# Lookup exponentials moved to GpSimd, and the layer-3 attention summary computed with values as weights in two 64-column tiles

## The reference, cut to what matters

```python
# L2F: product-key lookup of experts
h = silu(x @ W_up.T + b_up) @ W_down.T + b_down
q = (h @ W_q.T)...                        # 2 halves, 8 heads, 64 wide
sim = q . keys                            # 45 keys in each half
scores, idx = top_k(sim, 8)               # in each half
sc, pk = top_k(all 64 sums of a pair, 8)  # 8 experts in each of 8 heads
z = h . down_embed[indices]
z = silu(z * softmax(sc))
x = x + sum over heads, k of z * up_embed[indices]

# L3X: linear attention over the context; 16 heads of 16, 64 features
q', k' = relu(q @ Wqf.T), relu(k @ Wkf.T) * mask
kv, k_sum = sum over tokens of k' v, sum over tokens of k'
out = (q' kv) / (q' k_sum + 1e-8)
x = x + out @ Wo.T + bo
```

## Time and profile before

| | |
|---|---|
| median of 3 runs | 1339.32 us (1335.14 to 1339.72) |
| profiled execution, its time | 1336.76 us |
| its span | 1334.9 us |
| mean granted clock of TensorE | 0.919 of full speed |
| busy: TensorE, its weight loads | 1140.2 us (85%), 817.2 us (61%) |
| busy: DVE, ScalarE, GpSimd | 696.4 (52%), 482.1 (36%), 165.4 (12%) |
| this stage (L2F and L3X) | about 847 to 1161 us of the span |

### The profile page before, as it was taken

One profiled execution on the slowest core, in us unless ns is written; L12 is line 12 of the kernel. 1 busy time (PEld: TensorE's weight loads), 2 busy tenths in 40 slices (PEclk: granted clock), 3 DMA queues, 4 the chain that ended last, 5 costly groups with the idle time before them and its releaser, 6 DMA issues.

```text
span 1334.9 us, 22850 instructions
## 1 busy us (share of the span) xinstructions
PE 1140.2 (85%) x9353; PEld 817.2 (61%) x9353; DVE 696.4 (52%) x1532; ACT 482.1 (36%) x1069; POOL 165.4 (12%) x168
## 2 busy tenths in 40 slices
PE   6987889977877999999999977856986976777998
PEld 5866556656654555555556655735764755676886
DVE  3543456763326777655666253462626647374332
ACT  1101146762312355655566833222332321121322
POOL 0004000000001000000000000073635462000000
PEclk9998999998987999999999999977978957786999
DMA  9021200003003000000000020152524241003552
GB/s 365 1 95 48 111 1 1 2 2 154 0 16 135 1 2 2 1 2 1 2 2 2 2 77 1 54 145 63 152 70 123 78 113 48 14 0 158 198 204 81
DMA packets 16182, 84.38 MB, mean 63 GB/s; under 512 B 3152, under 2 KB 3664, under 8 KB 12368
## 3 DMA queue, kind: packets, MB, share of 16 engines
q1 hardware_dynamic: 7888, 57.75, 11.3%
q0 software_dynamic: 8192, 25.17, 6.7%
HBM read 82.65 MB, written 0.26 MB: 62 GB/s over the span
## 4 chain that ended last, share of the span: by engine, by line
PE 74%; DVE 12%; issue 5%; ACT 4%; another core or an unknown queue 3%; POOL 1%; DMA 1%; POOLq 0%; SPq 0%; DVEq 0%; ACTq 0%
PE L2X_bank_ring L1762 6%; PE L2X_bank_ring L1778 6%; PE L2X_bank_read L1792 5%; PE L2X_bank_ring L1701 4%; PE L2F_bank_sim L2389 3%; PE L1X_banks_scores L910 3%; PE L2X_bank_ring L1710 2%; PE L1X_bank_proj L887 2%; PE L0X_bank_k L457 2%; PE L2F_bank_keys L2347 2%; PE L3F_bank_y L3327 2%; PE L0X_bank_moments L468 2%; PE L2F_banks_pair L2364 2%; PE L3F_bank_gathered L3276 2%
## 5 line engine op out<-in xcount | busy, mean ns | idle before, releaser
L2059 DVE TENSOR_REDUCE L2X_max_parts<-L2X_bank_ring 128x1 f32<-128x512 f32 x256 | 158.3, 684 | 85.7 <-PE L2X_bank_ring L1762 85.7
L1970 ACT ACTIVATE L2X_context_exp<-L2X_bank_ring 128x384 f32<-128x384 f32 (+1 forms) x384 | 144.5, 465 | 62.1 <-PE L2X_bank_ring L1778 59.5
L2477 POOL DMA_INDIRECT L2F_rows<-in_L2F_embed_dram,L2F_expert x128 | 132.3, 1033 | 107.8 <-DVE x L2698 50.4
L1762 PE MATMUL L2X_bank_ring<-L2X_context_kT,L2X_q_masked 32*128 32x512 f32 x512 | 96.9, 630 | 0.0
L1016 ACT ACTIVATE L1X_probs<-L1X_clipped,L1X_drop,L1X_keep 128x1024 f32<-128x1024 f32 x64 | 77.9, 1240 | 32.1 <-DVE L1X_clipped L1075 24.9
L2389 PEld LDWEIGHTS L2F_bank_sim<-L3X_v_ones,L3X_k_features 128*128 128x128 f32 x512 | 72.1, 211 | 26.0 <-issue 24.2
L1075 DVE TENSOR_SCALAR L1X_clipped<-L1X_banks_scores 128x1024 f32<-128x1024 f32 x64 | 75.4, 1220 | 24.1 <-PE L1X_banks_scores L910 22.3
L2389 PE MATMUL L2F_bank_sim<-L3X_v_ones,L3X_k_features 128*128 128x34 f32 x512 | 69.2, 285 | 20.0 <-issue 19.8
L1778 PE MATMUL L2X_bank_ring<-L2X_q_and_max,L2X_context_kT 32*128 32x384 f32 (+1 forms) x768 | 86.0, 497 | 0.0
L1792 PEld LDWEIGHTS L2X_bank_read<-L2X_context_exp,L2X_context_v_ones 128*32 128x32 f32 x2048 | 50.2, 109 | 43.8 <-issue 33.4
L1792 PE MATMUL L2X_bank_read<-L2X_context_exp,L2X_context_v_ones 128*32 128x128 f32 x2048 | 75.8, 277 | 1.1 <-ACT L2X_context_exp L1970 0.8
(11 more groups left out here) (618 smaller groups left out, 2075.6 us busy)
## 6 DMA issues: line engine op xcount, KB each, us to landing
L3F_expert_weights<-in_L3F_experts_dram SPq DMA_DIRECT2D x16, 1280.0 KB, 5.6
L1A_groups<-in_L1A_groups_dram SPq DMA_DIRECT2D x3, 1536.0 KB, 9.6
ctxT<-in_ctxT_dram SPq DMA_DIRECT2D x8, 512.0 KB, 10.5
L0X_tokens<-in_L0X_tokens_dram SPq DMA_DIRECT2D x8, 512.0 KB, 15.0
slot<-in_L1A_dram SPq DMA_DIRECT2D x1, 3584.0 KB, 11.4
slot<-in_L0F_dram SPq DMA_DIRECT2D x1, 3072.0 KB, 11.0
slot<-in_L2A_dram SPq DMA_DIRECT2D x1, 3072.0 KB, 10.8
slot<-in_L2F_dram SPq DMA_DIRECT2D x1, 2476.5 KB, 9.7
```

The costliest lines, as they stand in the source:

```text
L1762: nc.tensor.matmul(bank[:, :], qm[32 * g:32 * g + 32, b, c, j, :], cT[32 * g:32 * g + 32, s % 3, blk * 512:(blk + 1) * 512], start=True, s ...
L1970: nc.scalar.activation(ex[:, n % NE, g, 0:width(s)], bank_of(s_e, done(n) + g + 1)[:, 0:width(s)], ACT.Exp, scale=SCALE).then_inc(s_e, 1)
L2059: nc.vector.tensor_reduce(parts[:, j, g, blk:blk + 1], bank_of(s_ft, n)[:, :], AX, ALU.max).then_inc(s_ft, 1)
L2477: pool.indirect_dma_start(out=rows[:, r, k, :], out_offset=None, in_=env.dram["L2F_embed"], in_offset=bass.IndirectOffsetOnAxis(idx[:, b, ...
```

## The change

1. GpSimd computes the exponentials of z and of the softmax of the second element, as powers of a constant exp(-1) (`per_e`): `tensor_tensor(..., ALU.pow)`. `exp_z(n-2)` stands after the fourth gather of chunk n. ScalarE keeps the first element's softmax at step 0. The sign of the shifted scores is turned for that.
2. The buffers of z, exp(z) and weights become three deep; DVE does `products(m)` before `weighted_sum(m-1)`.
3. The ring uses three buffers for nine chunks, then four. `choose(*parts[2])` moves to m = 6, `choose(*parts[3])` to m = 9; FRONT becomes 2.
4. `summary` has the 34 columns of values and ones of a pair as weights, in column tile 0 or 64 by turns, and moves the pair's 128 features. At an element's end ScalarE copies the bank (`copy_kv`), TensorE turns it (`turn_kv`, 4 transposes), and `kv_blocks` reads the turned form. Wv is packed so that pairs lie together.
5. TensorE no longer waits for the last `s_z`; 10 idle products instead of 24. The pieces 5 and 6 of element 0 move behind step 31, between those of element 1, and so do `divided(0)` and `add_out(0)` on DVE. `norm3` is split (`moments3`).

The diff, cut to its core:

```diff
-    ring = [0, 1, 2, 0, 1, 2, 3] + [n % 4 for n in range(len(chunks) - 7)]
+    ring = [n % 3 for n in range(9)] + [(n + 3) % 4 for n in range(len(chunks) - 9)]
...
-    FRONT, FINISH = 3, 25
-    exp_after = {1: 0, 4: 1, 6: 2, 8: 3, 13: 4, 16: 5, 17: 6, 21: 7, 23: 8, 25: 9, 26: 10, 27: 11, 29: 12, 31: 13}
+    FRONT, FINISH = 2, 25
...
-            vp = vo[:, n % NB, :].rearrange("p (a u c e) -> p a u c e", a=2, u=2, c=4)
             for j in range(NPAIR):
-                c, ct = divmod(j, 4)
-                i = nc.tensor.matmul(bank_kv[b][:, j * 2 * VW:(j + 1) * 2 * VW], kf[:, n % NB, j, :, :].rearrange("p r f -> p (r f)"),
-                                     vp[:, c, :, ct, :], start=(t == 0 and j == 0), stop=(t == NT - 1), skip_group_check=True)
+                lo, at = 64 * (j % 2), j // 2 * P
+                i = nc.tensor.matmul(bank_kv[b][lo:lo + 2 * VW, at:at + P], vo[:, n % NB, j * 2 * VW:(j + 1) * 2 * VW],
+                                     kf[:, n % NB, j, :, :].rearrange("p r f -> p (r f)"),
+                                     start=(t == 0 and j < 2), stop=(t == NT - 1), skip_group_check=True)
             i.then_inc(s_sum, 1)
+
+        def turn_kv(b):
+            pe.wait_ge(s_kvc, b + 1)
+            for j in range(NPAIR // 2):
+                i = nc.tensor.transpose(bank_kv[b][:, j * P:(j + 1) * P], kvT[:, j * P:(j + 1) * P], ident)
+            i.then_inc(s_kvt, 1)
...
-            finish(0, n - FINISH, bank_k, bank_k, (bank_k, bank_k), bank_k)
+            if n == NT + 4:
+                turn_kv(0)
+            if n - FINISH < 5:
+                finish(0, n - FINISH, bank_k, bank_k, (bank_k, bank_k), bank_k)
         summary(len(steps) - 1)
         pe.wait_ge(s_fc, len(steps))
-        pe.wait_ge(s_vc, len(steps))
-        pe.wait_ge(s_z, len(pieces))
-        idle_products(M, bank_v, 24)
-        for n in range(7):
-            finish(1, n, bank_x, bank_p0, (bank_p1, bank_h), bank_p0)
-            if n in (0, 4, 5):
-                idle_products(M, bank_v, 4)
+        idle_products(M, bank_v, 10)
+        finish(1, 0, bank_k, bank_k, None, bank_k)
+        turn_kv(1)
+        finish(1, 1, bank_k, bank_k, None, bank_k)
+        finish(0, 5, bank_kv[0], None, None, None)
+        finish(1, 2, None, None, (bank_p0, bank_p1), None)
+        finish(1, 3, None, None, (bank_p0, bank_p1), None)
+        finish(0, 6, None, None, None, bank_kv[0])
+        finish(1, 4, None, None, None, None)
+        idle_products(M, bank_v, 4)
+        finish(1, 5, bank_k, None, None, None)
+        idle_products(M, bank_v, 4)
+        finish(1, 6, None, None, None, bank_k)
...
+        nc.gpsimd.memset(per_e[:, :], float(np.exp(-1.0))).then_inc(s_base, 1)
...
+        def exp_z(m):
+            _, lo, hi = pieces[m]
+            pool.wait_ge(s_z, m + 1)
+            nc.gpsimd.tensor_tensor(ze[:, m % 3, lo:hi], per_e[:, lo:hi], zz[:, m % 3, lo:hi], ALU.pow).then_inc(s_ze, 1)
+
+        def exp_soft(part):
+            b, lo, hi = parts[part]
+            pool.wait_ge(s_sh, part + 1)
+            many = soft[:, b, lo:hi, :].rearrange("p h k -> p (h k)")
+            nc.gpsimd.tensor_tensor(many, per_e[:, 0:(hi - lo) * TOP], many, ALU.pow).then_inc(s_se, 1)
...
-            if n == 10:
-                rstd3[0].gpsimd(pool)
+                if k == TOP // 2 - 1:
+                    if chunks[n] in [p[0:2] for p in parts[2:]]:
+                        exp_soft([p[0:2] for p in parts].index(chunks[n]))
+                    if n == 10:
+                        rstd3[0].gpsimd(pool)
+                    if n >= 2:
+                        exp_z(n - 2)
+        for m in range(len(chunks) - 2, len(pieces)):
+            exp_z(m)
...
+        def copy_kv(b):
+            act.wait_ge(s_sum, NT * (b + 1))
+            act.wait_ge(s_zero, 1)
+            if b:
+                act.wait_ge(s_kvt, b)
+            for lo in (0, 64):
+                i = nc.scalar.activation(kvT[lo:lo + 2 * VW, :], bank_kv[b][lo:lo + 2 * VW, :], ACT.Copy)
+            i.then_inc(s_kvc, 1)
...
-        for m in range(len(pieces)):
-            if m == 4:
+        for m in range(len(pieces) + 1):
+            if m == 6:
                 natural_h(1, bank_e1)
                 choose(*parts[2], 5)
-            if m == 7:
+            if m == 9:
                 choose(*parts[3], 5)
...
-            products(m)
-            if m == 13:
-                divided(0)
-            weighted_sum(m)
-            if m == 14:
-                add_out(0, bank_k)
-                kv_blocks(1)
+            if m < len(pieces):
+                products(m)
+            if m:
+                weighted_sum(m - 1)
+            if m == 8:
+                moments3(0)
+            if m == 9:
+                norm3(0)
+        moments3(1)
         norm3(1)
+        divided(0)
+        kv_blocks(1)
+        add_out(0, bank_kv[0])
         divided(1)
-        add_out(1, bank_p0)
+        add_out(1, bank_k)
```

More of the change, by code:

```diff
@@ L2583, in _ @@
                 act.wait_ge(s_sh, 2)
[L2584 to L2590, removed]
+                nc.scalar.activation(soft[:, 0, :, :], soft[:, 0, :, :], ACT.Exp, scale=-1.0).then_inc(s_se, 1)
             if n % 4 == 0 and n // 4 + 1 < len(steps) // 4:
@@ L2593, in _ @@
             front(n - FRONT)
-            finish(0, n - FINISH, bank_k, bank_k, (bank_k, bank_k))
-        for m in range(len(exp_after), len(pieces)):
-            exp_z(m)
-        for n in range(7):
-            finish(1, n, bank_x, bank_p0, (bank_p1, bank_h))
+            if n == NT + 2:
+                copy_kv(0)
+            if n - FINISH < 5:
+                finish(0, n - FINISH, bank_k, bank_k, (bank_k, bank_k))
+        copy_kv(1)
+        finish(1, 0, bank_k, None, None)
+        finish(1, 1, None, bank_k, None)
+        finish(0, 5, bank_kv[0], None, None)
+        finish(1, 2, None, None, (bank_p0, bank_p1))
+        finish(1, 3, None, None, (bank_p0, bank_p1))
+        finish(1, 5, bank_k, None, None)
     @block.vector
@@ L2604, in _ @@
         head.vector(dve, chain)
+        nc.vector.memset(kvT[:, :], 0.0).then_inc(s_zero, 1)
         env.wait_weights(dve, "L2F")
@@ L2683, in products @@
             chain(nc.vector.tensor_tensor(down, down, hn[:, b, :].unsqueeze(1).to_broadcast([P, hi - lo, P]), ALU.mult))
-            chain(nc.vector.tensor_reduce(zz[:, m % 2, lo:hi], down, AX, ALU.add))
-            nc.vector.tensor_tensor(zz[:, m % 2, lo:hi], zz[:, m % 2, lo:hi], soft[:, b, h, lo:hi], ALU.mult).then_inc(s_z, 1)
+            chain(nc.vector.tensor_reduce(zz[:, m % 3, lo:hi], down, AX, ALU.add))
+            nc.vector.tensor_tensor(zz[:, m % 3, lo:hi], zz[:, m % 3, lo:hi], soft[:, b, h, lo:hi], ALU.mult).then_inc(s_z, 1)
         def weighted_sum(m):
@@ L2692, in weighted_sum @@
             dve.wait_ge(s_ze, m + 1)
-            chain(nc.vector.tensor_scalar(ze[:, m % 2, lo:hi], ze[:, m % 2, lo:hi], 1.0, None, ALU.add))
-            chain(nc.vector.reciprocal(ze[:, m % 2, lo:hi], ze[:, m % 2, lo:hi]))
+            chain(nc.vector.tensor_scalar(ze[:, m % 3, lo:hi], ze[:, m % 3, lo:hi], 1.0, None, ALU.add))
+            chain(nc.vector.reciprocal(ze[:, m % 3, lo:hi], ze[:, m % 3, lo:hi]))
             dve.wait_ge(s_z, m + 1)
-            chain(nc.vector.tensor_tensor(wt[:, m % 2, lo:hi], zz[:, m % 2, lo:hi], ze[:, m % 2, lo:hi], ALU.mult))
+            chain(nc.vector.tensor_tensor(wt[:, m % 3, lo:hi], zz[:, m % 3, lo:hi], ze[:, m % 3, lo:hi], ALU.mult))
             for k in range(lo, hi):
-                i = nc.vector.scalar_tensor_tensor(out=env.x[:, b, :], in0=rows[:, r, k, P:EMB], scalar=wt[:, m % 2, k:k + 1],
+                i = nc.vector.scalar_tensor_tensor(out=env.x[:, b, :], in0=rows[:, r, k, P:EMB], scalar=wt[:, m % 3, k:k + 1],
                                                    in1=env.x[:, b, :], op0=ALU.mult, op1=ALU.add)
@@ L2705, in _, with moments3, norm3 @@
         chain3 = Chain(dve, s_chain3)
-        def norm3(b):
+        def moments3(b):
             chain3(nc.vector.bn_stats(head.stats[:, b, :], env.x[:, b, :]))
             chain3(nc.vector.bn_aggr(head.mv[:, b, :], head.stats[:, b, :]))
-            rstd3[b].vector(dve, head.mv[:, b, 1:2], LN_EPS)
+            nc.vector.tensor_scalar(rstd3[b].sum[:, :], head.mv[:, b, 1:2], LN_EPS, None, ALU.add).then_inc(rstd3[b].s_sum, 1)
+        def norm3(b):
+            dve.wait_ge(rstd3[b].s_out, 1)
             nc.vector.tensor_scalar(xn[:, b, :], env.x[:, b, :], head.mv[:, b, 0:1], rstd3[b].out[:, 0:1],
@@ L2760, in _ @@
                 normalise(*parts[2], 2)
-                norm3(0)
             if m == 12:
```

31 lines of the change are left out of this document (14 added, 17 removed).

## The result

The changed kernel takes 1284.38 us (median of 4 runs, 1281.4 to 1285.12) against 1339.52 us for the kernel before, run beside it: a ratio of 0.9579, 95% interval 0.9535 to 0.9624. The profiled span falls from 1334.9 to 1282.9 us, 52.0 less, and the stage of L2F and L3X (845.3 to 1109.1 after, 263.8 us, against 847.0 to 1161.1, 314.1 us) holds 50.3 of them.

What follows compares the result with a forecast made beforehand. The prediction took the attention stream, slowed during gathers, as the bound: 154.2 us of work plus loss, mean end 1122, plus 15 us tail gives 1137 instead of 1161.1; 1336.8 - 24 = 1313 us, range 1278 to 1350.

Steps and rivals of the forecast that it cites:

- What bounds the kernel: In stage L2F and L3X: lookups and attention stream wait on each other; 81.9 of the stream's 255.7 us are lost.
- coupled chains: Lookups wait for ScalarE's exponentials (DVE 78.9 us), which come only at fixed steps of the attention stream.
- crawl: Attention stream (TensorE, ScalarE) nearly stops about 18 us into long gather series, running at factor 0.29; cause unknown.
- Powers: Exponentials moved to GpSimd: 1.7 us per 8 columns, 38 us in all; waiting for DVE's products costed at nothing.
- Summary: Attention stream's summary matmuls: 1.18 instead of 1.80 us per step, 19.8 us off the stream over 32 steps.
- Tail: Stage's end after the last summary: 15 us, or about 17 if the lookups end last; 18 before.
- The loss: Stream time lost during gathers, 81.9 us before, carried over to the changed kernel; mean stream end 1122.
- four laws: Four ways to carry the stream's loss over: 82, 100, 95 or 122 us, ending it at 1104, 1122, 1117 or 1144.
- Law (a): Stream loss proportional to gathering, share 0.48: 82 us with powers counted as relief, 100 as load.
- The first: Rival: lookups, not the stream, end last, at 1095; stage 49 us shorter, 1288 us; chance 0.20.
- Rival 2: Slower: uninterrupted gather series make one long crawl, pauses of 1.7 us don't help; 1351 to 1364 us; chance 0.17.
- Instruction fetch: Possible cause of the stream's crawl: engines stream instructions by DMA in 16 KiB blocks; unproven, no size given.

Runs made afterwards that it cites:

- e1: Kernel before plus 16 GpSimd powers of 8 columns that nobody reads, one after the fourth gather of each chunk; 1285.11 us, ratio 0.9574.
- e4: Changed kernel with the old summary put back, powers still on GpSimd; 1284.72 us, ratio 0.9577 to the kernel before.
- e2: Changed kernel with its GpSimd powers replaced by plain multiplications or additions of the same shapes; 1324.3 us, ratio 0.9863 to the kernel before.
- e5: Kernel before with each gather moving 256 instead of 384 columns of a row (131 instead of 197 KB); 1337.27 us, ratio 0.997.
- e6: Changed kernel with plain operations for powers, GpSimd waiting before each chunk until the previous chunk's gathers landed; 1281.89 us, ratio 0.9566 to the kernel before.
- e11: Kernel before with only a GpSimd wait added before each chunk's first gather until the previous 8 gathers landed; 1295.59 us, ratio 0.9677.

## Why the prediction was wrong, step by step

*What bounds the kernel.* Right as far as it went: coupled chains, and a crawl that matters more than any operation. e1 sharpens it: removing the crawl alone is worth 57 us, the coupling with it left in.

*Powers.* 1.67 us for 8 columns (1.42 + 0.3 = 1.7 forecast) and 5.45 for 32 (4.3 forecast, 2.3 us too little in all): the slope grows to 0.16 us per column. GpSimd paces with 12.4 us per chunk, against 12.3. GpSimd's wait for DVE's products, put at nothing, was 3.9 us at the first power and 5.5 at the last. For the rule of the Trainium skill (SBUF — State Buffer, section "SBUF: two separate sides") that GpSimd and DVE exclude each other on a shared port pair I had looked at the weighted sums. There the traces don't agree: their median is 485 ns in both kernels, the longest of the 128 records 506 and 515, and one power of the usual 1.67 us (at 1018.86) ran beside them (one line's duration, min/median/max in ns, of the changed kernel):

```profile
L2736 DVE SCALAR_TENSOR_TENSOR x<-L2F_rows,L2F_expert_weight,x x128: 483/485/515, 898.1 to 1094.1; 128x256 f32<-128x256 f32 x128
```

For DVE's multiplication of the down rows, which also reads two SBUF tensors, they do agree, and it is GpSimd that pays: what it begins during that multiplication ends late. The first power, begun 0.18 us behind one, took 2.57 us instead of 1.67:

```profile
894.65 1.22 DVE L2721 TENSOR_TENSOR L2F_rows<-L2F_rows,L2F_h 128x1024 f32<-128x1024 f32 x1
```

In the kernel before, all 12 gathers that begin during it took 1.24 to 2.00 us, where the median of the 128 is 0.95. In e1, where the crawl is gone, gathers and powers end late in the same way, so this is not the crawl.

*Summary.* 0.80 us per step instead of 0.62, inside its bounds (up to 0.9). But its 19.8 us were counted into the result, and they were worth nothing there (e4): with the lookups last, the stream's work is cover.

*Tail.* 14.4 us; 15 or 17 forecast.

*The loss.* This is the step that failed. I carried the loss over in proportion to gathering, or at factor 0.29 after 18 us of a series, with the powers as load or as time without gathers: 82 to 122 us. None of the four laws let a pause of 1.7 us inside a series end the crawl. Measured: the stream's work is now 32 x 3.13 + 31.4 + 5.5 + 14.3 + 1.0 - 0.8 = 151.6 us, it would end at 867 + 152 = 1019 and ended at about 1064, so 45 us are lost, part of them in the 25 us before the first power. So the stream ended 31 us before the lookups, and with the loss fell the forecast's order, the stream last. Law (a) with powers as relief came nearest and was still 37 too high: a share averaged over series without such pauses says nothing of what a pause does. One series did have a pause inside, and I counted it as one long series: the second of the four breaks off at 954.1 and goes on with 16 gathers after 1.99 us,

```profile
956.08 0.95 POOL L2477 DMA_INDIRECT L2F_rows<-in_L2F_embed_dram,L2F_expert  x1 [1.99 <-PE L2F_bank_sim L2276]
```

and its stretch in the earlier trace rows was the mildest, a factor 0.49. I had the row that said more: ScalarE went on right after the gathers paused. A stall that ends with the pause asks what a short pause does; I let it bound nothing.

*The rivals.* The first came true in who ends last and in its time: first series to 962 (963.6), gathers again at 979 (971), end of the lookups 1095 (1094.6), x at 1112 (1109.1), 1288 us (1284). Part of that is luck. The choice, its reason for 979, was made by 962.8; what held GpSimd until 971 was the weighted sum behind it in DVE's queue, which frees the row buffer. From there to the end of the lookups it took 123.7 us, not 116, the wait of 5.5 at the last power among them, so two misses of some 8 us cancel. Its chance, 0.20, was too small: its condition was a crawl milder than in (a), and what spoke for it, powers that break up the series, was the decisive fact. Rival 2 stood for a series without pauses, and e2 built that: the crawl came, its 1351 us did not (1324).

*Instruction fetch.* By the Trainium skill (Runtime: NRT & Kernel Launch, section "Instruction fetch mechanics") engines fetch their instructions by DMA in blocks; one starved of them should then go on when a block arrives. The DMA queues of the kernel before in the crawl and 6 us behind it, 888 to 918 us (packets, MB, share):

```profile
q0 software_dynamic: 1109, 3.37, 39.6%
```

No packet of an instruction queue, while TensorE and ScalarE stalled and went on at 912. The crawl of e2 behaved so too, 908 to 942 us:

```profile
q0 software_dynamic: 1622, 5.00, 51.1%
```

The one instruction packet inside ScalarE's stall there (891.4 to 936.0) came at 905, and ScalarE stood for 30 us more. So a late block is not what they waited for.

**What stays open.** Which resource the dense gathers take. Excluded, as far as these runs go, are bytes, a quarter of the packets and a third of the DMA engines' load (e5), instruction blocks (by the queues of the traces), and the operation on GpSimd (e6). That it is the rows fetched, or the signals of the gathers, is only argued. No run varied the number of rows per gather.

## What to carry to other kernels

Where one engine issues gathers without a pause for tens of us, look at what the *other* engines do meanwhile: records per us in stretches, and "issue" or "remote" waits that end when the issuing does. Break such a series up before moving any work; here a pause of 1.7 us every 8 gathers, or a wait until they have landed, was worth 42 to 57 us (e1, e11, e6 against e2). And an operation added to an engine is not only load: ask what its place in the queue interrupts, and give it a price of either sign.

## What the hardware showed that was not expected

Indirect gathers of 128 rows issued every 1.25 us slowed the stream of TensorE and ScalarE, whose steps wait for none of the gathered rows, down to 1.3 records per us over 75 us (e2), with one ScalarE stall of 44.6 us; in the 40 us without gathers TensorE ran at 6.8. The DMA engines were half busy then, and with a third fewer bytes a third, to no effect. A pause of 1.67 us, or 2.8 us idle, per 8 gathers lifted the stream to 4.6 to 5.4 records per us; 0.6 per 8, or 2.94 per 16, brought 11 and 17 us instead of 42 to 57. A power on GpSimd took 1.67 us for 8 columns and 5.45 for 32. A power or gather that GpSimd began during DVE's multiplication of 128x1024 ended late, by up to 1.05 us; the one power of the changed kernel beside DVE's weighted sums of 128x256 took its usual 1.67.
